# Gated cross-attention and FFN on one core: attention output normalised, biased and split on GpSimd inside the attention stage

## What is computed

```python
def xattn(query, key, value):                      # key = value = ctx
    Q, K, V = heads(query, Wq, bq), heads(key, Wk, bk), heads(value, Wv, bv)
    scores = Q @ K.T / sqrt(32) + adj              # per batch and head, 1024 x 1024
    scores = where(mask == 0, -inf, scores)
    out = softmax(scores) @ V
    return merge_heads(out) @ Wo.T + bo

def ffn(x):
    gf = sigmoid(mlp3(x.mean(axis=1)))             # one number per batch
    out = x
    for _ in range(3):                             # cycles
        tf = sigmoid(mlp4(out))                    # 512 -> 512 -> 256 -> 128 -> 1
        coupling = 0.1 + adaptive_range * (0.7 * gf + 0.3 * tf - 0.5) * 2.0
        out = out + coupling * twist(out)          # twist permutes and negates four blocks of 128
    return out

x = x + tanh(g_xattn) * xattn(layernorm(x), ctx, ctx)
x = x + tanh(g_ffn) * ffn(layernorm(x))
```

## Time and profile before

| | us |
|---|---|
| median of 3 runs (lowest, highest) | 1894.16 (1892.35, 1894.46) |
| the profiled execution's own time | 1890.45 |
| its span, first to last instruction | 1888.8 |
| stage 1 in the span | 0 to 293 |
| stage 2 | 293 to 1286 |
| stage 3 | 1286 to 1889 |

### The profile page before, as it was taken

The page is one execution under the profiler, slowest core; times in us unless marked ns, Lnnn a source line. Parts: engine busy times, 40 slices in busy tenths (PEclk is TensorE's granted clock), DMA queues, the critical chain, the costliest instruction groups (busy, mean ns, idle before and its releaser), DMA issues. The chain is left out here.

```text
span 1888.8 us, 33975 instructions
## 1 busy us (share of the span) xinstructions
PE 1774.0 (94%) x12280; PEld 1279.9 (68%) x12280; DVE 1514.1 (80%) x2524; ACT 1243.0 (66%) x2154; POOL 536.6 (28%) x476
## 2 busy tenths in 40 slices
PE   8999998999999999999999999994898998998995
PEld 6888886777777777777777777773644744744742
DVE  6455547999999999999999999993758858768757
ACT  3222226999999999999999999992543452552542
POOL 3424332111382111831108511103423223222111
PEclk9999998999999999999999999997999999999997
DMA  7766776331466132752316633107120320320101
GB/s 266 261 230 249 264 233 127 79 69 49 104 191 108 49 85 76 199 115 64 80 41 193 141 79 79 35 10 218 45 89 0 104 89 5 98 89 19 40 1 44
DMA packets 122012, 203.91 MB, mean 108 GB/s; under 512 B 11600, under 2 KB 64080, under 8 KB 121872
## 3 DMA queue, kind: packets, MB, share of 16 engines
q1 hardware_dynamic: 78640, 122.58, 19.4%
q0 software_dynamic: 42128, 77.36, 18.6%
q10 hardware_dynamic: 1104, 2.10, 0.3%
HBM read 143.01 MB, written 58.98 MB: 107 GB/s over the span
## 5 line engine op out<-in xcount | busy, mean ns | idle before, releaser
L754 DVE CUSTOM_DVE_ANT_0 a_neg<-a_sc_ps,am 128x1024 f32<-128x1024 f32 x512 | 620.6, 1212 | 2.5 <-PE a_sc_ps L607 2.5
L703 ACT ACTIVATE a_prob<-a_neg,a_row_min 128x1024 f32<-128x1024 f32 x512 | 587.0, 1147 | 10.6 <-DVE a_row_min L754 7.5
L619 PEld LDWEIGHTS a_tr_ps<-a_ident,a_prob 128*128 128x128 f32 x4096 | 461.4, 141 | 134.4 <-issue 100.3
L619 PE MATMUL a_tr_ps<-a_ident,a_prob 128*128 128x128 f32 x4096 | 546.3, 276 | 1.4 <-ACT a_probT L683 1.4
L729 DVE COPY a_probT<-a_tr_ps 128x512 f32<-128x512 f32 x512 | 353.5, 690 | 48.6 <-PE a_tr_ps L619 36.5
L683 ACT ACTIVATE a_probT<-a_tr_ps 128x512 f32<-128x512 f32 x512 | 305.6, 597 | 72.1 <-PE a_tr_ps L619 48.1
L550 POOL DMA_DIRECT2D a_q_st<-q_parts x144 | 78.0, 549 | 443.8 <-PE a_sc_ps L607 439.3
L1170 PE MATMUL f_acc<-f_u,f_w 128*128 128x512 f32 x384 | 175.7, 602 | 11.8 <-ACT f_u L1310 11.8
L1170 PEld LDWEIGHTS f_acc<-f_u,f_w 128*128 128x128 f32 x384 | 73.0, 193 | 107.5 <-issue 85.4
L640 PE MATMUL a_o_ps<-a_probT,v_first 128*32 128x256 f32 x2048 | 137.0, 385 | 0.0
L640 PE MATMUL a_o_ps<-a_probT,a_v 128*32 128x256 f32 x2048 | 136.4, 385 | 0.2 <-ACT a_probT L683 0.2
(11 more groups left out here) (211 smaller groups left out, 2918.0 us busy)
## 6 DMA issues: line engine op xcount, KB each, us to landing
a_q_st<-q_parts POOLq DMA_DIRECT2D x144, 128.0 KB, 2.8
k_first<-k_parts POOLq DMA_DIRECT2D x24, 512.0 KB, 7.3
a_k_st<-k_parts POOLq DMA_DIRECT2D x24, 512.0 KB, 7.5
a_m_raw<-mask SPq DMA_DIRECT2D x24, 512.0 KB, 5.0
a_adj_raw<-adj SPq DMA_DIRECT2D x24, 512.0 KB, 5.9
p_x_raw<-x POOLq DMA_DIRECT2D x8, 1024.0 KB, 7.2
k_parts<-p_out_hi SPq DMA_DIRECT2D x32, 256.0 KB, 4.1
k_parts<-p_out_lo SPq DMA_DIRECT2D x32, 256.0 KB, 5.9
```

What stands on the lines that cost most here:

```text
L619: last = pe.transpose(tr_ps[:, half, j * P:(j + 1) * P], prob[:, r % NPROB, t * P:(t + 1) * P], ident[:])
L703: act.activation(prob[:, r % NPROB, :], neg[:, r % 2, :], ACT.Exp, scale=-1.0, bias=row_min[:, r % 2:r % 2 + 1], accum_out=row_sum[:, r // ...
L754: dve.tensor_tensor_reduce(out=neg[:, r % 2, :], in0=sc_ps[:, r % 2, :], in1=am[:, 2 * qb + qt, :], scale=-1.0, scalar=3.4e38, op0=ALU.add ...
```

## The change

1. **Attention output.** New helpers `load_weighted`, `split_weighted`, `store_weighted` handle a piece of 128 features by 512 tokens, 32 pieces in all. SP loads o and 1/sum. POOL multiplies them and splits with four operations of its own (a multiplication by 4097 and three subtractions). SP stores the parts to DRAM (`att_parts`). 28 pieces are done within stage 2, three to four groups behind the attention itself. The last 4 (`LATE`) are done in batch 0 of stage 3, by POOL behind `split_pair(0, 1, 1)`. Stage 3 then only loads the parts (`load_attention`, on POOL's queue). bv is added to V in stage 1, on the copy out of PSUM, which becomes an addition.
2. **x + gated bo** is made by POOL in stage 2, in eight steps, and stored to DRAM (`x_bo`). tanh(g_xattn) and the gated bo are made by ACT and DVE at the head of stage 2.
3. **Wo** is split by POOL in stage 2. The first layer's weights and the first parts of X are loaded near the end of stage 2.
4. **The beta product of B** in cycle 2 moves from POOL to DVE, into `mix`.
5. **ACT's order** within a turn: `h3_all` and `gate` move ahead of most of the h1 tiles.
6. **Loops.** Stage 3's batches and POOL's loop of stage 1 are unrolled. K, Q and V of the first group are loaded in the middle of stage 1. Stage 1 no longer waits for its last stores: stage 2 waits for those that it reads. Tiles get fixed SBUF addresses (`Placer`), so that some live across stages.

```diff
+def load_weighted(sp, w, n):
+    G, half = n // 2, n % 2
+    b, g = G // (H // HPG), G % (H // HPG)
+    sp.wait_ge(w.step, 5 * n)
+    for parity in range(2):
+        sp.wait_ge(w.o_stored[parity], 16 * (n + 2))
+    sp.wait_ge(w.rinv_stored, 16 * (G + 2))
+    at = b * S + half * CH
+    sp.dma_start(w.o[:], w.o_all[g * P:(g + 1) * P, at:at + CH]).then_inc(w.loaded, 16)
+    for h in range(HPG):
+        row = h * (S // P) + half * TT
+        sp.dma_start(w.rinv[h * D:(h + 1) * D], w.rinv_all[G, row:row + TT, :].rearrange("q s -> (q s)").partition_broadcast(D)
+                     ).then_inc(w.loaded, 16)
+
+
+def split_weighted(pool, w, n):
+    pool.wait_ge(w.loaded, 80 * (n + 1))
+    pool.tensor_tensor(w.o[:], w.o[:], w.rinv[:], ALU.mult).then_inc(w.step, 1)
+    wait(pool, w.stored, 32 * n)
+    pool.wait_ge(w.step, 5 * n + 1)
+    pool.tensor_scalar(w.lo[:], w.o[:], SPLITTER, 0.0, ALU.mult, ALU.add).then_inc(w.step, 1)
+    pool.wait_ge(w.step, 5 * n + 2)
+    pool.tensor_tensor(w.hi[:], w.lo[:], w.o[:], ALU.subtract).then_inc(w.step, 1)
+    pool.wait_ge(w.step, 5 * n + 3)
+    pool.tensor_tensor(w.hi[:], w.lo[:], w.hi[:], ALU.subtract).then_inc(w.step, 1)
+    pool.wait_ge(w.step, 5 * n + 4)
+    pool.tensor_tensor(w.lo[:], w.o[:], w.hi[:], ALU.subtract).then_inc(w.step, 1)
+
+
+def store_weighted(sp, w, n):
+    G, half = n // 2, n % 2
+    b, g = G // (H // HPG), G % (H // HPG)
+    at = b * S + half * CH
+    sp.wait_ge(w.step, 5 * n + 5)
+    for part, tile in enumerate((w.hi, w.lo)):
+        sp.dma_start(w.parts[part, g * P:(g + 1) * P, at:at + CH], tile[:]).then_inc(w.stored, 16)
...
-            with pool.Fori(1, NCH) as c:
+            for c in range(1, NCH):
+                if c == 4:
+                    first_group()
...
-            for m in range(ET):
-                sp.wait_ge(stored[m], 64 * NCH)
-            sp.wait_ge(v_stored, 16 * NCH)
...
-                    dve.tensor_copy(v_out[:, m, :], acc[:, m, :]).then_inc(acc_read, 1)
+                    dve.tensor_tensor(v_out[:, m, :], acc[:, m, :], bv_rows[:], ALU.add).then_inc(acc_read, 1)
...
+        X_SLOTS = (2, 4, 6, 8, 10, 12, 27, 43)
+        WO_SLOT, WO_BEHIND = 59, 24
+        SLOTS = NG * NQB + 2
+
+        def weighted_at(n):
+
+            G, i = n // NQB, n % NQB
+            if G < 3 or G % GPB == 0 and G < NG:
+                return None
+            if G == NG:
+                return 2 * (NG - 3) + i
+            if G % GPB == 1:
+                return 2 * (G - 4) + i
+            if G % GPB == 2:
+                return 2 * (G - 3) + i if i < 2 else None
+            return 2 * (G - 3) + i - 2 if i >= 2 else None
...
+            def load_x(c):
+                wait(sp, x_bo_stored, 16 * c)
+                wait(sp, weighted.stored, 32 * sum(weighted_at(n) is not None for n in range(X_SLOTS[c])))
+                sp.dma_start(st_rows[:], rows(x, c)).then_inc(st_loaded, 16)
+
+            def store_x(c):
+                sp.wait_ge(bo_added, c + 1)
+                sp.dma_start(rows(x_bo, c), st_rows[:]).then_inc(x_bo_stored, 16)
+
+            def load_wo():
+                sp.wait_ge(weighted.stored, 32 * WO_BEHIND)
+                sp.dma_start(wo_raw[:], WoT.rearrange("(t p) f -> p t f", p=P)).then_inc(wo_loaded, 16)
...
+                if t + 2 in X_SLOTS:
+                    store_x(X_SLOTS.index(t + 2))
+                if weighted_at(t + 2) is not None:
+                    store_weighted(sp, weighted, weighted_at(t + 2))
+                if t + 4 in X_SLOTS:
+                    load_x(X_SLOTS.index(t + 4))
+                if t + 4 == WO_SLOT:
+                    load_wo()
+                if t + 4 < SLOTS and weighted_at(t + 4) is not None:
+                    n = weighted_at(t + 4)
+                    wait(sp, x_bo_stored, 16 * sum(slot < t + 4 for slot in X_SLOTS))
+                    if n == WO_BEHIND:
+                        sp.wait_ge(wo_step, 4)
+                    load_weighted(sp, weighted, n)
+            sp.wait_ge(sc_ready, UG * (NG - 1) + 2 * UB)
+            sp.dma_start(w1_raw[:], cn_w1.rearrange("(t p) f -> p t f", p=P)).then_inc(w1_loaded, 16)
...
+            def load_first_attention():
+
+                pool.wait_ge(sc_ready, UG * (NG - 1))
+                pool.wait_ge(weighted.stored, 32 * 2 * GPB)
+                for part, tile in enumerate((X0_hi, X0_lo)):
+                    pool.dma_start(tile[:], weighted.parts[part, :, 0:CH].rearrange("(t p) s -> p t s", p=P)).then_inc(X0_loaded, 16)
...
+                if n in X_SLOTS:
+                    add_bias(X_SLOTS.index(n))
+                if n == WO_SLOT:
+                    split_wo()
+                if n == NG * NQB:
+                    load_first_attention()
+                if weighted_at(n) is not None:
+                    split_weighted(pool, weighted, weighted_at(n))
...
+            act.wait_ge(bo_loaded, 32)
+            act.activation(gate_x[:], gate_x[:], ACT.Tanh).then_inc(gate_ready, 1)
...
+            dve.wait_ge(gate_ready, 1)
+            dve.tensor_scalar(gated_bo[:], gated_bo[:], gate_x[:], None, ALU.mult).then_inc(bo_ready, 1)
...
-            body(0, True, True)
-            with eng.Fori(1, B - 1) as b:
-                body(b, False, True)
-            body(B - 1, False, False)
+            for b in range(B):
+                body(b, b == 0, b < B - 1)
...
+                if first:
+                    for n in range(LATE, 2 * B * GPB):
+                        load_weighted(sp, weighted, n)
+                        store_weighted(sp, weighted, n)
+                    sp.wait_ge(weighted.stored, 32 * 2 * B * GPB)
+                else:
                     store_y(b - 1, 1)
                 if more:
-                    sp.wait_ge(x1_ready, NJ * TT * (b + 1))
-                    load_weighted(b + 1, 0, o_raw)
-                    load_rinv(b + 1, 0, rinv)
-                    sp.wait_ge(att_ready, ET * (NJ * (b + 1) + 1))
-                    load_weighted(b + 1, 1, o_raw)
-                    sp.wait_ge(att_lo_ready, ET * (NJ * (b + 1) + 1))
-                    load_rinv(b + 1, 1, rinv)
-                    load_x(b + 1, 0)
-                    load_x(b + 1, 1)
+                    for j in range(NJ):
+                        if not first:
+                            sp.wait_ge(x1_ready, TT * (NJ * b + j + 1))
+                        load_x(b + 1, j)
...
+            def load_attention(b, j):
+
+                wait(pool, product_ready, 4 * ET * (NJ * (b - 1) + j + 1) if b else 0)
+                pool.wait_ge(weighted.stored, 32 * 2 * GPB * (b + 1))
+                for part, tile in enumerate((X_hi[j], X_lo[j])):
+                    src = weighted.parts[part, :, b * S + j * CH:b * S + (j + 1) * CH].rearrange("(t p) s -> p t s", p=P)
+                    pool.dma_start(tile[:], src).then_inc(X_loaded[j], 16)
+
+            load_attention(0, 1)
...
-            def normalise_attention(b, j):
-                pool.wait_ge(o_loaded[j], 16 * (b + 1))
-                pool.wait_ge(rinv_loaded[j], 16 * HPG * (b + 1))
-                pool.tensor_tensor(rinv[:], o_raw[:], rinv[:], ALU.mult).then_inc(att_ready, ET)
-
-            def add_bias(b, j):
-                pool.wait_ge(x_loaded[j], 16 * (b + 1))
-                pool.tensor_tensor(x_before(b)[j][:], x_before(b)[j][:], gated_bo[:].unsqueeze(1).to_broadcast([P, TT, E]),
-                                   ALU.add).then_inc(xbo_ready, 1)
...
+                if first:
+                    for n in range(LATE, 2 * B * GPB):
+                        split_weighted(pool, weighted, n)
                 if more:
-                    normalise_attention(b + 1, 0)
-                    normalise_attention(b + 1, 1)
-                    add_bias(b + 1, 0)
-                    add_bias(b + 1, 1)
-                for j in range(NJ):
-                    pool.wait_ge(coef_step, coef_steps(b, 1, j))
-                    for m in range(ET):
-                        pool.tensor_tensor(Bt[j][:, m, :], Bt[j][:, m, :], beta[:, j, :], ALU.mult).then_inc(B_scaled, 1)
...
-                    if s == 0:
-                        pe.wait_ge(att_lo_ready, ET * (NJ * b + j) + t + 1)
+                    if s == 0 and t == 0:
+                        pe.wait_ge(X_loaded[j], 32 * (b + 1))
...
+            act.wait_ge(small_loaded, 16 * 12)
             act.activation(gate_x[:], gate_x[:], ACT.Tanh).then_inc(gate_x_ready, 1)
-            split_attention(0, 0, rinv)
-            split_attention(0, 1, Bt[1])
-            act.wait_ge(small_loaded, 16 * 11)
             act.activation(gate_f[:], gate_f[:], ACT.Tanh).then_inc(gate_f_ready, 1)
...
                     if between:
                         h1(*other, 0)
-                        h1(*other, 1)
-                    if k == 0 and more:
-                        split_attention(b + 1, 1, rinv, (0, 1))
                     h3_all(b, n, j)
                     if between:
+                        h1(*other, 1)
```

(9 more changed lines are left out.)

420 lines of the change are left out of this document (203 added, 217 removed).

## The result

The changed kernel takes 1835.73 us (median of 4 runs, 1833.06 to 1837.46), the kernel before 1893.26 us beside it (4 runs). The ratio is 0.9693, 95% interval 0.9677 to 0.9710: 3.1% faster. The profiled execution's span went from 1888.8 to 1831.3 us, 57.5 us less.

What follows compares the result with a forecast made beforehand. PE was taken as full in stage 2, stage 3 as a chain of waits. Terms -20.4 - 42.1 + 3.0 + 1.0 + 0.8 = -57.7 took 1890.45 to 1832.8 us, 1836.5 against the median; range 1822 to 1863.

Steps and rivals of the forecast that it cites:

- Turns, -42.1: Stage 3's coupling turns: layer 2 of turn 0 to layer 3 of turn 5 at PE's pace, 55.2 us; gain 42.1 us.
- The two causes named for cycle 2: POOL's products of B slow DVE's operations to 1.75 us; h3 behind two h1 tiles makes PE wait 1.9 us.
- the third for turn 0: POOL's product with 1/sum for the next batch runs mid-turn 0, leaving ACT and DVE splits between their turns' work.
- the rival that cycle 2 keeps its pace: Stage 3 turns: DVE slightly late every turn, gain 14.1 us instead of 42.1, time 1864.5; chance 0.20, wholly or half.
- Head of stage 3, -20.4: Start of stage 3: first residual 17.1 us sooner, plus 3.3 from POOL's addition to x; gain 20.4 us.
- gate and second x at about 1303: Head of stage 3: 4.2 MB take 15 us plus some 2.5, so the first residual's inputs land near 1303.
- Last four pieces, +3: Batch 0 of stage 3: POOL's last 10 splitting operations hold DVE in the turns, 0 to 11 us, taken as 3.
- Stage 1 to 2, +1.0 and +0.8: Boundary: loss of 1.0 us waiting for gate and bo loads; 0.8 us for bv's load ahead of stage 1's first x.
- 291.3 + 0.8 + 4 + 0.7: Stage 2's start: first row minimum at 296.8, with the load taken as 4 us and 0.7 us of work.
- Stage 2, 0: POOL's about 237 us of added work beside DVE in stage 2 costs nothing, and SP's store of o stays on time.
- The mask rows: Profile rows with POOL busy 39.8 of 62 us instead of 6.5, DVE still doing 101 operations in 59.2 us.
- 2038: Rival time in us: POOL and DVE exclude each other in stage 2, costing 201 us; chance of slower 0.04.

Runs made afterwards that it cites:

- kernels 1 to 4: The changed kernel with B's product back on POOL: 1847.2 us; ACT's old order: 1839.0; both: 1861.4; the kernel before with only these two edits: 1867.0.
- kernel 8: The changed kernel with the attention gate's load first, on its own semaphore, the other eleven small loads waited for only where used: 1831.74 us.
- Kernel 5: The changed kernel with tanh of the gate and the product with bo moved behind the first units of stage 2: 1828.04 us.
- kernels 9 and 10: The changed kernel with POOL's four splitting operations per stage 2 piece doubled: 1853.75 us; the same with most stores of o on ACT's queue: 1836.85 us.

## Why the prediction was right, and where it was not

The time was forecast as 1836.5 us and came out at 1835.7, and the sum of terms, -57.7, stands against -57.5 measured. The largest term and the mechanism behind it were right. That the sum is met to 0.2 us is luck: the start and the boundary were 3.3 us worse than summed and the head 1.4 worse, while turns and last pieces together were 2.3 better and 2.1 came from between the batches, which no term had. One of the prediction's own signs of being wrong did appear, the first row minimum behind 300 (it came at 300.89), and the first residual came at 1310.8 and not near 1303.

- **Turns, -42.1: right, -41.4.** PE's own pace of 55.2 us is 55.4 in batches 1 to 3 (55.6 in batch 0), since the later turns take 9.76 us of PE rather than 9.63. The margin of 0.2 us on DVE is in the trace as 0.20. The two causes named for cycle 2 and the third for turn 0 were each shown (kernels 1 to 4). That the two in cycle 2 reinforce each other was not foreseen. Without both edits the rival that cycle 2 keeps its pace would have come true, and without one of them a part of it.
- **Head of stage 3, -20.4: right in kind, 1.4 too large.** The sum of the two head stretches is -19.0. Of the 20.4, PE's start was right: it came 0.9 us behind the end of stage 2, whose place in the span had moved by 5 us. The step that failed is "gate and second x at about 1303", 18 us behind the start: the residual came after 20.8. The working priced bytes at 0.28 MB/us and took the gate's place behind X as the bound. The bulk went at up to 0.38 MB/us, and the gate did land sooner, 15.9 us behind PE's start. But the wait was for the last of twelve small loads, 20.5 us behind it, and x itself was there 13 us before the residual (kernel 8). So the two errors nearly met.
- **Last four pieces, +3: too much, +0.2.** The collisions came as described. In batch 0's turn 1, coefficient and multiplications were held beside POOL, and in the first layer, where DVE reads PSUM, they were not (timeline of POOL, then of DVE):

```profile
1351.61 1.30 POOL L110 TENSOR_TENSOR st_o<-st_o,st_rinv 128x512 f32<-128x512 f32 x1
...
1389.29 1.27 POOL L115 TENSOR_TENSOR st_hi<-st_lo,st_o 128x512 f32<-128x512 f32 x1
```

```profile
1351.86 0.69 DVE L1528 TENSOR_TENSOR f_B<-f_B,f_acc 128x512 f32<-128x512 f32 x1 [1.23 <-PE f_acc L144]
...
1389.41 1.44 DVE L1538 TENSOR_SCALAR f_beta<-f_coef,f_range,f_base 128x512 f32<-128x512 f32 x1 [3.20 <-ACT f_coef L1408]
1390.88 3.31 DVE L1562 TENSOR_TENSOR f_u<-f_B,f_beta 128x512 f32<-128x512 f32 x2
```

 Only the last two rounds met DVE's work, the third for 1 us and the fourth for 3 (0.9 and 2.0 us in the two rows above), and DVE had 3.20 us of idle time ahead of it: the slack was there.
- **Stage 1 to 2, +1.0 and +0.8: the term that was mis-sized, +5.1.** The 0.8 for bv is met in this execution (0.0 to 1.0 in the others'). "291.3 + 0.8 + 4 + 0.7" failed in two places. The block started at 293.3, since stage 1 ended 1.7 us later and the store wait that was dropped saved just that. And bo took 6.0 us to land, not 4, issued at 294.19, behind the gate's load, ahead of 1 MB of x on the same queue and beside POOL's six loads of Q. Which of these made it longer was not tried. Kernel 5 gives these 6.1 us back. Of stage 1's 1.7 us, 0.9 are the early first group, which I had called covered "beside a PE that is full": they stood ahead of the next chunk's loads.
- **Stage 2, 0: right for the reason given, with a bound that I had not priced.** The mask rows were the right ones to read. The Trainium skill, SBUF — State Buffer, Who interferes with whom, says that a DVE instruction with at most one SBUF input does not contend with GpSimd outside its two-port modes, that one with two SBUF inputs does, and that `tensor_scalar` can enter such a mode. The traces agree in all three: 1213 ns for the row minima with POOL doubled, 1.75 us instead of 0.68 for two SBUF inputs, 1.44 instead of 0.55 for the `tensor_scalar` above. The sentence weighed in the prediction (the Trainium skill, Perfetto Trace Analysis) names the exclusive lock of a two-port operation but gives no condition on operands; read alone it would have meant 2038. What does bound the move is SP's queue (kernels 9 and 10). I had `store_o` as "on time" because it stands "ahead of both". It does so in its own slot, but it stands behind the waits of the slot before. It is on time in the changed kernel, and doubling POOL's pieces uses up its slack.
- **Between the batches: -2.1 was in no term.** The clock explains little of it. The stretch from batch 1 to batch 2 has it at 1.00 throughout in both kernels, and is 0.6 us shorter all the same (columns as in the earlier trace rows; the kernel before, then the changed one):

```profile
1589.63:1662.69 73.06, 67.62 (x317) 53.41 (x317) 57.83 (x120) 33.45 (x65) 13.37 (x13) 1.00 0.27 82
```

```profile
1551.04:1623.49 72.45, 67.09 (x317) 53.38 (x317) 55.11 (x115) 31.00 (x61) 10.47 (x14) 1.00 0.32 97
```

 PE's waits are as long (5.4 us), but its 317 matmuls take 0.5 us less. They follow one another a little closer all through the stretch. No run was made for it, and why stays open.

No run bears on the unrolling apart, since no changed kernel with the loop was run. In the kernel before, the stretch over the loop's branch (73.06 us) is no longer than the two others (73.53 and 73.09).
